# Transformer loop: feed-forward product split over heads 4 and 5, first value product at head 6, second product at head 7, one gelu for all columns

## What is computed

```
def _expert(x, Wqkv, bqkv, Wo, bo, g1, be1, W1, bf1, W2, bf2, g2, be2):
    qkv = x @ Wqkv.T + bqkv
    q, k, v = (to_heads(t) for t in split(qkv, 3))             # 8 heads of 32
    attn = softmax(einsum('bhqd,bhkd->bhqk', q * scale, k))    # over all 1354 tokens
    ctx = einsum('bhqk,bhkd->bhqd', attn, v) @ Wo.T + bo
    x = _layernorm(x + ctx, g1, be1)
    h = gelu(x @ W1.T + bf1)                                   # 1024 hidden features
    h = gelu(h @ W2.T + bf2)
    return _layernorm(x + h, g2, be2)
```

## Time and profile before

| | |
|---|---|
| median of 3 runs | 3071.9 us (3063.94 to 3073.24) |
| profiled execution | 3070.8 us |
| its span | 3069.0 us |
| mean granted clock, whole program | 0.899 |
| TensorE busy, whole program | 2453.9 us, 80% |
| VectorE busy | 1550.3 us, 51% |
| ScalarE busy | 1154.3 us, 38% |
| transformer loop | about 1640 to 2720 us |

### The profile page before, as it was taken

One profiled execution on the slowest core, in us unless ns is written; L12 is line 12 of the kernel. 1 busy time (PEld: TensorE's weight loads), 2 busy tenths in 40 slices (PEclk: granted clock), 3 DMA queues, 4 the chain that ended last, 5 costly groups with the idle time before them and its releaser, 6 DMA issues. The chain is left out here.

```text
span 3069.0 us, 52763 instructions
## 1 busy us (share of the span) xinstructions
PE 2453.9 (80%) x18627; PEld 2037.6 (66%) x18627; DVE 1550.3 (51%) x3095; ACT 1154.3 (38%) x2240; POOL 521.4 (17%) x818
## 2 busy tenths in 40 slices
PE   6979689769977849975785999999999989964256
PEld 4858579769965744764784777777777777754244
DVE  3636522232235751143444777777777767742355
ACT  2333212111212321121223666666666656624433
POOL 0000022122212110510001222222222212110043
PEclk8989789869978969977997999999999999976578
DMA  5000022124332120320665231234254452112223
GB/s 127 1 7 1 19 87 84 65 90 133 107 80 73 55 90 35 118 71 22 226 258 175 72 110 38 75 110 128 68 142 135 113 143 67 26 50 48 83 67 106
DMA packets 133799, 268.82 MB, mean 88 GB/s; under 512 B 33378, under 2 KB 70280, under 8 KB 130468
## 3 DMA queue, kind: packets, MB, share of 16 engines
q1 hardware_dynamic: 114740, 212.77, 22.3%
q0 software_dynamic: 18800, 52.69, 6.5%
HBM read 461.01 MB, written 65.74 MB: 172 GB/s over the span
## 5 line engine op out<-in xcount | busy, mean ns | idle before, releaser
L2239 PE MATMUL tx_ring<-g_ident,tx_p 128*128 128x128 f32 x2552 | 401.4, 284 | 53.9 <-DVE tx_p_t L2484 20.4
L2239 PEld LDWEIGHTS tx_ring<-g_ident,tx_p 128*128 128x128 f32 x2552 | 286.8, 142 | 165.4 <-DVE tx_p_t L2484 57.1
L2477 DVE TENSOR_REDUCE tx_neg_max<-tx_scores 128x1 f32<-128x1354 f32 x232 | 361.0, 1556 | 16.2 <-PE tx_scores L2227 16.1
L2373 ACT ACTIVATE tx_p<-tx_scores,tx_neg_max 128x1354 f32<-128x1354 f32 x232 | 322.3, 1389 | 88.2 <-DVE tx_neg_max L2477 85.5
L2484 DVE COPY tx_p_t<-tx_ring 128x512 f32<-128x512 f32 x464 | 301.2, 679 | 46.4 <-PE tx_ring L2239 46.3
L2380 ACT ACTIVATE tx_p_t<-tx_ring 128x384 f32<-128x384 f32 x232 | 113.1, 488 | 272.9 <-PE tx_ring L2239 269.3
L2227 PE MATMUL tx_scores<-tx_keys,tx_queries 96*128 96x512 f32 (+1 forms) x696 | 202.8, 400 | 15.6 <-DMA tx_queries<-tx_q_hi 11.2
L2279 PE MATMUL tx_ring<-tx_p_t,tx_values 128*32 128x128 f32 x5104 | 152.0, 274 | 18.3 <-ACT tx_p_t L2380 17.8
L2279 PEld LDWEIGHTS tx_ring<-tx_p_t,tx_values 128*32 128x32 f32 x5104 | 135.9, 110 | 29.4 <-ACT tx_p_t L2380 28.9
L2227 PEld LDWEIGHTS tx_scores<-tx_keys,tx_queries 96*128 96x128 f32 x696 | 115.9, 193 | 27.0 <-issue 16.5
L192 PE MATMUL ln_turned<-g_ident,g_xn 128*128 128x128 f32 x176 | 38.6, 402 | 117.3 <-DVE g_xn L179 117.3
(11 more groups left out here) (958 smaller groups left out, 5281.4 us busy)
## 6 DMA issues: line engine op xcount, KB each, us to landing
tx_keys<-expert_keys SPq DMA_DIRECT2D x696, 169.5 KB
lv1e_w<-in_L_ffn_W SPq DMA_DIRECT2D x232, 256.0 KB
tx_w<-in_L_ffn_W SPq DMA_DIRECT2D x58, 1024.0 KB
lv0e_w<-in_L_ffn_W SPq DMA_DIRECT2D x200, 256.0 KB
tx_values<-expert_values SPq DMA_DIRECT2D x58, 704.0 KB
tx_rows<-in_L_ffn_rows SPq DMA_DIRECT2D x29, 640.0 KB, 3.9
g_adj_t<-in_adj_t POOLq DMA_DIRECT2D x3, 3872.0 KB, 22.9
expert_values<-kv_v SPq DMA_DIRECT2D x8, 1408.0 KB, 5.7
```

Source lines behind the costliest of these rows:

```text
L2239: last = nc.tensor.transpose(ring[u % 2][:, (t - t0) * P:(t - t0 + 1) * P], p[n % 2][:, t * P:(t + 1) * P], g.ident[:])
L2373: nc.scalar.activation(p[n % 2][:, 0:N], sc[n % 2][:, 0:N], ACT.Exp, bias=neg_max[:, n % 4:n % 4 + 1], accum_out=row_sum[:, i % 2, hd:hd + ...
L2477: nc.vector.tensor_reduce(neg_max[:, n % 4:n % 4 + 1], sc[n % 2][:, 0:N], AX_X, ALU.max, negate=True)\
```

## The change

The order of work behind the heads changes on all engines. Behind head 4 stands the first half of the first product of the tile before, behind head 5 its second half, behind head 6 the inverses and first values of this tile, behind head 7 the second product. In head 5, as in head 6, the scores now stand between the first and second group of turns. ScalarE drains the halves with an Identity that adds the bias, and in head 6 one gelu runs in place over all 1024 columns of `h` (`bend`), then the result's gelu, then the copy of the inverses; the second product waits for `h_done`. VectorE does both parts of the end norm and the addition to the second product in head 7. Seven turned heads are kept in place of five, because the values of heads 0 to 3 are now mixed after head 6; the two exponent buffers move to memory of an earlier stage to make room.

```
-TURNED = 5
-PE_EXTRAS = {0: ("inverse1", "values1"), 1: ("turn_rows", "output"), 2: ("queries",), 3: ("turn_middle",), 4: ("inverse0", "values0"),
-             5: ("first0", "first1"), 6: ("second",)}
+TURNED = 7
+PE_EXTRAS = {0: ("inverse1", "values1"), 1: ("turn_rows", "output"), 2: ("queries",), 3: ("turn_middle",), 4: ("first0",), 5: ("first1",),
+             6: ("inverse0", "values0"), 7: ("second",)}
...
-        p = [s.sb(f"p{i}", [P, NP]) for i in range(2)]
+        p = [nc.alloc_sbuf_tensor_at(f"tx_p{i}", [P, NP], F32, offset=g.slab + 4 * NP * i) for i in range(2)]
...
             def second(i):
                 u = at["second", i, 0]
                 free(pe, u)
-                written(pe, at["first1", i, 0])
+                pe.wait_ge(h_done, i + 1)
...
-                        if hd != 6:
+                        if hd not in (5, 6):
                             turn(i, hd, 1)
                         if HEADS * i + hd + AHEAD < heads:
                             scores(HEADS * i + hd + AHEAD)
-                        if hd == 6:
+                        if hd in (5, 6):
                             turn(i, hd, 1)
...
             def hidden(i, part):
                 u = at[f"first{part}", i, 0]
                 act.wait_ge(full, u + 1)
+                if i and part == 0:
+                    act.wait_ge(full, at["second", i - 1, 0] + 1)
                 for f in range(4):
                     t = 4 * part + f
-                    last = nc.scalar.activation(h[:, t, :], ring[u % 2][:, f * P:(f + 1) * P], ACT.Gelu,
+                    last = nc.scalar.activation(h[:, t, :], ring[u % 2][:, f * P:(f + 1) * P], ACT.Identity,
                                                 bias=cols[:, i % SMALL, KD + t:KD + t + 1])
                 last.then_inc(drained["act"], 1)
+
+            def bend(i):
+                written(act, at["first1", i, 0])
+                nc.scalar.activation(h[:], h[:], ACT.Gelu).then_inc(h_done, 1)
...
-                    if hd == 4 and i < tiles:
-                        keep_inverse(i, 0)
-                    if hd == 5:
+                    if hd == 4 and 0 < i <= tiles:
+                        hidden(i - 1, 0)
+                    if hd == 5 and 0 < i <= tiles:
+                        hidden(i - 1, 1)
+                    if hd == 6:
                         if 0 < i <= tiles:
-                            hidden(i - 1, 0)
+                            bend(i - 1)
                         if i >= 2:
                             result(i - 2)
-                        if 0 < i <= tiles:
-                            hidden(i - 1, 1)
+                        if i < tiles:
+                            keep_inverse(i, 0)
...
-                    if hd == 4 and i < tiles:
+                    if hd == 6 and i < tiles:
+                        inverse(i, 1)
                         context(i, 0)
-                    if hd == 5 and i >= 2:
-                        end_stats(i - 2)
-                    if hd == 6:
+                    if hd == 7:
                         if i >= 2:
+                            end_stats(i - 2)
                             end_norm(i - 2)
                         if 0 < i <= tiles:
                             add_second(i - 1)
-                        if i < tiles:
-                            inverse(i, 1)
```

More of the change, by code:

```diff
@@ L2096, in stage_attend_tiles @@
         drained = {"act": s.sem("drained_act"), "dve": s.sem("drained_dve")}
-        exp_done, q_done, gelu_done = (s.sem(n) for n in ("exp_done", "q_done", "gelu_done"))
+        exp_done, q_done, h_done, gelu_done = (s.sem(n) for n in ("exp_done", "q_done", "h_done", "gelu_done"))
         v_step, max_done, q_scaled, q_split, inv_made, ctx_done, x1_seen, x1_n_done, x2_seen, z_done = (
@@ L2349, in _ @@
                         turn_middle(i - 1)
-                    if hd == 4 and i < tiles:
+                    if hd == 4 and i:
+                        first(i - 1, 0)
+                    if hd == 5 and i:
+                        first(i - 1, 1)
+                    if hd == 6 and i < tiles:
                         turn_inverse(i, 0)
                         mix(i, 0)
[L2353 to L2356, removed]
+                    if hd == 7 and i:
                         second(i - 1)
@@ L2958, in program @@
         at = slab(nc, s, "normed", CHOICES * NB * D)
+        g.slab = at
         g.xn = nc.alloc_sbuf_tensor_at("g_xn", [P, NB, D], F32, offset=at)
```

## The result

| | before | after |
|---|---|---|
| median | 3071.9 us (3063.94 to 3075.33, 9 runs) | 3082.5 us (3078.79 to 3088.8, 9 runs) |
| span of the profiled execution | 3069.0 us | 3087.1 us |
| ratio of the times | | 1.0037, 95% interval 1.0027 to 1.0047 |

The change makes the kernel slower by 10.6 us; forecast were 36. It is slower by just over the 0.3% that a measurement can tell from nothing. The forecast mechanism is in the trace, at less than half its forecast size.

The account below looks back on a forecast made before the run. TensorE was taken to set the loop's time. 27 x 1.2 = 32.4, plus 2.9 in tile 0 and 2.4 in the last tile, made 37.7 on 3070.8: 3108 us, range 3070 to 3142.

Parts of the forecast that it names:

- the walk: Step-by-step timing of one tile after the change, from head 4 to the next tile's head 1: loss 1.2 us.
- 27 x 1.2 = 32.4: The 27 tiles that stack queries behind a full tile lose 1.2 us each, 32.4 in all.
- I take 2067.7 as the time when the queries are ready: Head 6: the stacked queries are there then, so TensorE waits 1.8 us before the next tile's scores.
- 3090: Estimate in us with some 2.0 us fixed time per stacking DMA: queries ready at 2067.0, loss 0.5 a tile.
- the inverses behind the gelu: Head 6 on ScalarE: their copy follows the gelu, so head 7 starts 0.5 us after the value product.
- Tile 0: Once only: the value product and its inverses come behind the 4.28 us wait for queries, costing 2.9 us.
- The tail: Last tile, once: nothing hides the table load and gelu before the second product, costing 2.4 us.
- Better balance: Rival: the second product lies over waits in heads 6 and 7, gaining 1.07 us a tile, 3041 us; chance 0.12.
- The clock: Rival: the granted clock falls after head 6's wait, costing 27 x 2 us more, 3162 us; chance 0.09.
- Loads: Rival: weight loads nearer the stacking delay queries 2.9 us at up to 7 expert changes, 3128 us; chance 0.08.
- Queries early enough: Rival: in head 6 only the banks make TensorE wait, 5.3 us in all, to 3080 us; chance 0.07.
- The table load: Rival: on ScalarE it costs another 1.28 us on the path, 28 times, 36 us, 3144 us; chance 0.02.

Follow-up runs that it names:

- experiment 1: GpSimd splits the queries before it adds the middle rows, in both kernels: changed kernel 3068.95 us, ratio 1.0007; kernel before 3069.53 us, 1.0002.
- experiment 2: GpSimd does the subtraction for `q_lo` twice, in both kernels: changed kernel 3097.86 us, ratio 1.0098; kernel before 3074.0 us, 1.0018.
- experiment 7: Kernel before with Identity drains and one gelu in head 5, end statistics moved to head 6: 3125.24 us, ratio 1.0107.
- experiment 4: Changed kernel with queries split before the middle rows, `q_hi` stacked before `q_lo` is made, inverses copied before the gelu: 3086.46 us, ratio 0.9972.
- experiment 6: Kernel before with both halves drained by Identity and one gelu in head 5, end statistics left there: 3221.96 us, ratio 1.0413.

## Why the prediction was right in kind and wrong in size

**Right.** The direction; the place of the wait (the next tile's scores in head 6, in 25 of 28 tiles); its cause, shown by experiments 1 and 2: with the first issue 1.4 us earlier the wait was gone and a tile took 36.5 again, with the queries 0.56 later a tile took 0.54 more; TensorE's arrival, 8.6 us after the first stacking DMA by the walk and 8.77 in the trace; the gelu of 1024 columns, 1.10 and 1.06; heads 1 to 3 unchanged.

**The step that failed** is the term 27 x 1.2 = 32.4. A tile lost 0.62 us by the medians (36.55 to 37.17), not 1.2, which would make 16.7; and over the 26 tiles of the two traces only 9.7, since the long tiles of the kernel before were not in those of the changed one. The sum had carried them over with its 3070.8, as if the change left them alone. In the 1.2 the first error is the sentence "I take 2067.7 as the time when the queries are ready". On its clock that is 10.4 us after the first issue. In the trace after it is 9.07 to 10.28, mostly near 10.0: the issues take 8.4 and the last DMA is there 1.36 after they have ended, some 2.0 after its own issue. I had one landing of 3.1 and let it outweigh the minimum of 1.8 and the median of 2.3. In the trace after, the issues between 2105.0 and 2107.3 landed in 1.9 us. The Trainium skill, DMA: Bandwidth & Descriptors, section Anatomy of one DMA, gives some 2.0 us of fixed time, told of DMAs issued from GpSimd. The 1.9 agrees with that, and the estimate that the prediction made by it, 3090, was nearer than its sum. This shift is 0.4 of the 0.6 us a tile by which I was too high.

The other part is the inverses behind the gelu. Head 7 was to start 0.5 us after the value product; the trace has about 0.2. From the scores to the next head 1 it took 16.04 us where the walk had 16.3.

**The wait is not the loss.** Behind tile 0 the waits before the scores are 0.26 to 1.26 us, 0.83 in the mean of the tiles from the fourth on. A tile with 0.35 takes 36.54, one with 1.26 takes 37.44 or 37.46: 0.3 us of each wait is free, since the turns behind it would otherwise have stood for a bank that ScalarE's Identities still held (0.18 in the row of head 5). The walk had this too: TensorE stood before the scores at 2065.94, and queries ready before 2066.3 were to cost 0 to 0.1. So the free part was right, and what it was taken from was not.

**Tile 0** was to lose 2.9 us and lost 0.65 in these two traces. The wait did stay, 4.51 us, but the queries were there at 1665.95, not 1667.83. I had moved the product behind a fixed landing. One pair of traces doesn't settle this term, though: the scores in head 6 of tile 0 started 11.3 to 14.0 us after the first stacking DMA over the twelve traces, in either order. Tile 0 took 33.3 to 35.6 us in the six with the old order and 35.8 to 38.7 in the six with the new one, 34.5 and 37.6 in the median. That difference is near the 2.9; the 0.65 is luck. Why the landing varies no run here shows.

**The tail** was to lose 2.4 and lost 3.9. The rows after, and then those of before:

```profile
2722.03 0.41 PE L2298 MATMUL tx_ring<-g_ident,tx_x_n 128*128 128x128 f32 x2 [3.12 <-DVE tx_x_n L2537]
2723.38 6.56 PE L2310 MATMUL tx_ring<-tx_x_t,tx_w 128*128 128x128 f32 x32 [0.94 <-ACT tx_x_t L2422]
2732.30 5.38 PE L2320 MATMUL tx_ring<-tx_w,tx_h 128*128 128x256 f32 x16 [2.37 <-issue]
```

```profile
2711.41 5.43 PE L2310 MATMUL tx_ring<-tx_x_t,tx_w 128*128 128x128 f32 x32 [0.94 <-ACT tx_x_t L2421]
2718.11 3.69 PE L2320 MATMUL tx_ring<-tx_w,tx_h 128*128 128x256 f32 x16 [1.28 <-ACT tx_h L2430]
```

The wait before the second product grew by only 1.1 us, from 1.28 to 2.37. The rest is clock: the first product takes 1.1 us longer (granted clock 0.56 from 2723 to 2730, where it was 0.72 from 2711 to 2717 before), the second 1.7. This rest is not the change's alone. In experiment 2's trace of the changed kernel the two took 5.35 and 3.69 us, in experiment 1's trace of the kernel before the first took 6.76.

**The rivals.** *Better balance* didn't decide in the changed kernel, but it is no phantom: with the queries in time it offsets the whole cost of one gelu (experiments 1 and 7), and with the inverses ahead it wins (4). *The clock* stayed at 0.99 as a whole and fell in two of 27 tiles. They take 38.7 us, 1.4 more than tiles with the same wait. TensorE's rows in one of them, and a window before the fall and one at it:

```profile
2368.63 0.86 PE L2227 MATMUL tx_scores<-tx_keys,tx_queries 96*128 96x512 f32 x3 [1.12 <-issue]
...
2370.71 0.48 PE L2266 MATMUL tx_ring<-g_ident,tx_inv_rep 128*128 128x128 f32 x1 [0.46 <-DVE tx_p_t L2493]
2371.11 4.07 PE L2279 MATMUL tx_ring<-tx_p_t,tx_values 128*32 128x128 f32 x88
```

```profile
2369.00:2370.00 1.00, 1.00 (x10) 0.95 (x8) 0.04 (x1) 0.62 (x2) 0.00 (x0) 1.00 0.02 8
2370.00:2372.00 2.00, 1.54 (x24) 1.02 (x26) 2.00 (x2) 1.70 (x2) 0.00 (x0) 0.68 0.00 0
```

The value product takes 4.07 us instead of 2.61. A wait of 1.12 stood before it; tiles with 1.26 kept their clock. So the length of that wait alone doesn't decide, and what does stays open. *Loads*: no wait behind tile 0 is longer than 1.26 us, so the collision that I feared isn't there. *Queries early enough* came about in three of 27 tiles, which took 36.51 or 36.52 us. *The table load* took 1.28 us as before, and the gelu started 0.02 us after its end (2111.73 + 1.28 and 2113.03).

## What to carry to other kernels

When work is moved behind a point that waits for a DMA, count the slack from the end of the queue's last issue, over all repetitions, and give the input a lead before moving anything: here the reordering of two GpSimd steps was worth nearly as much as the change lost. Look for the baseline's own rare waits before multiplying one tile by 27: here they were worth 6 us. And don't price a term that stands once by one pair of traces. Price a wait by what it displaces as well as by its length. And an edit that delays one engine's result needs every reader of that result looked at, as experiment 6 shows: a reader that was early enough before now blocks its own queue.

## What was not expected of the hardware

- A VectorE copy of 128x128 in SBUF took 0.54 us beside a GpSimd subtraction and 0.23 without (experiment 2), in nearly every tile.
- After a wait of 3.73 us the granted clock was 0.61 over 4 us, and the second product took 5.41 us instead of 3.72 (experiment 6); after one of 1.12, followed by one of 0.46, it fell in two tiles of 27 (0.68 over 2 us in one, 0.67 over 4 us in the other), while it stayed at 1.00 in others with a wait as long.
- VectorE drained 512 columns of PSUM with the addition of a broadcast bias in 0.69 us, as long as its plain copy of the same size. ScalarE needs 1.14 for four pieces of 128.
- Twelve issues of 32 KB from SyncE took 7.7 to 8.9 us in the changed kernel's loop. Two groups of four took 2.5 to 2.6 us in most tiles, and one of the three often 3.2 to 3.8; the cause of the longer one was not found.
